# The down projection of an attention and feed-forward kernel: Strassen's seven products on 16 of its 22 inner tiles, instead of eight plain ones

## The chip, the core and the metric

One core of one Trainium2 chip. The metric is the device time of one execution in microseconds. Below, PE is TensorE, DVE is VectorE, ACT is ScalarE, POOL is GpSimd and SP is SyncE, which here only issues DMAs.

## The reference

```
xn = layernorm(x)                                    # x: 2 x 1024 tokens, width 1024, f32
s  = attention(xn, wq, wk, wv, wo)                   # 32 heads, 8 kv heads; s = (attended values) @ wo
w_gu, w_d = dequant(4-bit words, zeros, scales)      # 1024 x 5504 and 2752 x 1024
gate, up = split(xn @ w_gu)
h  = silu(gate) * up                                 # 2048 tokens x 2752
out = x + s * silu(h @ w_d)                          # h @ w_d is the down projection
```

## The kernel before, in words

Every f32 matrix product is done in f16 with each operand split into a high part and a low remainder: high x high, high x low and low x high, three matmuls of 128 x 128 by 128 x 512 where one would stand. All matmuls accumulate in PSUM in f32.

There are three stages. The first (`project_qkv`) normalises and projects; the second (`attend_and_expand`) does attention, dequantises, computes h and stores to scratch memory the transposed h (`ht_d`, f16 high and low), the dequantised w_d (`wd_d`, f16 high and low, 22 inner tiles of 128 rows, the last of 64) and the attention sums (`o_d`). The third is `finish`, the subject here. It loops over TT = 16 token tiles of 128 rows, the result of one being 128 x 1024 in two halves of BANK = 512 columns.

Each engine has its own program, executed in the order in which it is written out; semaphores are waited for with `wait_ge`. For token tile n (in the code m = n // 2, u = n % 2), `finish` does:

- DVE `dve_normalise` (L1820 to L1832): reciprocal of the row sums, an addition of the two parts of the attention sums, a multiplication, and a 32 x 32 block transposition. Then ACT `act_high` (L1770) makes the f16 high part of it, and DVE `dve_low` (L1841) the remainder.
- PE `project` (L1717): 8 inner tiles x 3 x 2 halves = 48 matmuls with wo. ACT `take` (L1786) brings the result from PSUM to SBUF, where it stays.
- PE `down` (L1731, L1726): for each half, 21 x 3 + 2 = 65 matmuls of h with w_d, which lies in SBUF as a whole (`wd_a` to `wd_e`).
- ACT `gate` (L1793): silu from PSUM. DVE `weigh` (L1859): times s. POOL `total` (L1899; for the last tile DVE, L1866): plus x. SP stores the half or the tile.

The order on PE: project 0, 1, 2; then the down products of tiles 0 and 1 inner tile by inner tile, while the weights arrive; project 3; and then in turn tile n (130 matmuls) and project n + 2 (48). So ACT and DVE prepare one projection in the time of 178 matmuls. `tail` puts the preparation of the first projections into the end of the second stage. All DMAs of the stage are issued by SP, in program order, each behind the waits ahead of it.

The buffers of `finish` lie in memory that the earlier stages used (`xT`, `stock`, `room`, `arena`), and two semaphore groups tell it when these are free: `units_done` and `units_stored`.

## Time and profile before

| | us |
|---|---|
| median of 3 runs | 2242.79 (2242.72 to 2243.02) |
| the profiled execution, own time | 2242.64 |
| its span | 2240.9 |
| TensorE busy | 2220.2 |
| VectorE busy | 1221.9 |
| GpSimd busy | 1200.0 |
| ScalarE busy | 930.6 |

The profile is one execution. Matmuls are pipelined, so that the duration of a single one (379 ns) is longer than the distance to the next; distances are read from blocks of them, count and time. A group's mean is over its instructions, and contains what they waited for while running. The chain of waits starts at the last instruction and goes back to what released each one.

### The profile page before, as it was taken

What the parts mean: (1) busy time and instruction counts of PE and PEld (TensorE: products, weight loads), DVE (VectorE), ACT (ScalarE), POOL (GpSimd) and SP (SyncE); (2) the same over time, 40 slices, a digit from 0 to 9 for tenths busy, and PEclk for the clock granted to TensorE, in tenths of its full rate; (3) what the DMA queues carried; (4) which work ended last, traced back from release to release, by engine and by line L of the source; (5) the groups of instructions that cost most, each with busy time, mean ns of one, the idle gap of its engine ahead of it and who ended that gap; (6) DMA issues with size and microseconds to landing.
All of it is one profiled execution on the core that took longest, in us unless ns stands there. A gap on an engine that the chain in (4) does not pass through costs nothing.

```text
span 2240.9 us, 38593 instructions
## 1 busy us (share of the span) xinstructions
PE 2220.2 (99%) x15048; PEld 1125.2 (50%) x15048; DVE 1221.9 (55%) x1951; ACT 930.6 (42%) x1806; POOL 1200.0 (54%) x1318
## 2 busy tenths in 40 slices
PE   7999999999999999999999999999999999999999
PEld 4555545555555555555555555444444444444444
DVE  5677677777777777777777763345312211112100
ACT  4333156666666666666666665332201000000000
POOL 4855588887887888788888876333301101001000
PEclk9999999999999999999999999999999999999999
DMA  7344212443424433334443233533273222313120
GB/s 208 97 105 100 50 33 57 72 76 55 67 59 81 72 67 59 67 62 72 76 61 61 66 53 61 94 103 92 81 295 127 100 91 77 113 64 127 45 89 19
DMA packets 266666, 188.03 MB, mean 84 GB/s; under 512 B 189728, under 2 KB 236318, under 8 KB 264052
## 3 DMA queue, kind: packets, MB, share of 16 engines
q1 hardware_dynamic: 266484, 185.56, 34.8%
q8 instruction: 119, 1.95, 0.4%
q14 instruction: 63, 0.52, 0.1%
HBM read 113.47 MB, written 71.90 MB: 83 GB/s over the span
## 4 chain that ended last, share of the span: by engine, by line
PE 98%; ACT 1%; DVE 0%; issue 0%; POOL 0%; DMA 0%; DVEq 0%; ACTq 0%; POOLq 0%
PE gu_ps L1174 39%; PE dn_ps L1731 19%; PE qk_ps L722 9%; PE out_ps L1717 7%; PE mx_ps L1071 6%; PE sc_ps L1115 6%; PE o_ps L1137 4%; PE v_ps L705 2%; PE o_ps L1141 2%; PE sz_ps L1084 2%; PE sz_ps L1089 1%; PE dn_ps L1726 1%; PE tr_ps L691 1%; ACT L1223 0%; POOL xl L412 0%
## 5 line engine op out<-in xcount | busy, mean ns | idle before, releaser
L1174 PE MATMUL gu_ps<-xT,wg 128*128 128x512 f16 x4128 | 983.6, 378 | 0.0
L1505 POOL TENSOR_TENSOR room<-room 128x1152 f16<-128x1152 f32 x256 | 539.5, 2107 | 40.3 <-ACT room L1223 26.4
L1174 PEld LDWEIGHTS gu_ps<-xT,wg 128*128 128x128 f16 x4128 | 367.8, 97 | 377.2 <-issue 0.7
L1223 ACT ACTIVATE room<-sc_ps 128x512 f32<-128x512 f32 (+3 forms) x768 | 349.3, 489 | 368.7 <-PE sc_ps L1115 365.0
L1731 PE MATMUL dn_ps<-xT,hT_in 128*128 128x512 f16 x1536 | 336.2, 379 | 0.0
L1899 POOL TENSOR_TENSOR room<-room 128x512 f32<-128x512 f32 x30 | 51.2, 1710 | 530.0 <-DVE room L1859 530.0
L1859 DVE TENSOR_TENSOR room<-room 128x512 f32<-128x512 f32 x32 | 23.9, 752 | 415.6 <-ACT room L1793 415.5
L1731 PEld LDWEIGHTS dn_ps<-xT,hT_in 128*128 128x128 f16 x1536 | 150.3, 98 | 181.2
L1500 POOL TENSOR_SCALAR_AFFINE_SELECT room<-room 128x128 f32<-128x128 f32 x512 | 144.8, 299 | 140.4 <-ACT room L1223 140.4
L1350 DVE TENSOR_REDUCE shift<-mx_ps 128x2 f16<-128x1024 f32 (+3 forms) x256 | 212.8, 831 | 8.8
L722 PE MATMUL qk_ps<-xT,w 128*128 128x512 f16 x960 | 212.8, 379 | 0.0
L1115 PE MATMUL sc_ps<-arena 97*128 97x512 f16 (+3 forms) x768 | 209.7, 327 | 2.3 <-ACT room L1223 2.1
L1350 DVE TENSOR_REDUCE part<-mx_ps 128x2 f16<-128x1024 f32 x128 | 157.1, 1227 | 100.3 <-PE mx_ps L1071 100.3
L1793 ACT ACTIVATE room<-dn_ps 128x512 f32<-128x512 f32 x32 | 19.0, 597 | 415.5 <-PE dn_ps L1726 415.2
L1137 PE MATMUL o_ps<-arena,room 128*128 128x65 f16 x2240 | 191.1, 191 | 0.0
L1071 PE MATMUL mx_ps<-arena 96*128 96x512 f16 (+3 forms) x768 | 188.0, 325 | 0.6 <-DVE shift L1350 0.6
L1141 PE MATMUL o_ps<-arena,room 128*128 128x33 f16 x2304 | 184.1, 178 | 0.0
L1137 PEld LDWEIGHTS o_ps<-arena,room 128*128 128x128 bf16 x2240 | 160.7, 97 | 32.4
L1717 PE MATMUL out_ps<-room,arena 128*128 128x512 f16 x768 | 168.1, 379 | 0.0
L1141 PEld LDWEIGHTS o_ps<-arena,room 128*128 128x128 f16 x2304 | 148.6, 96 | 37.5
L1345 DVE TENSOR_TENSOR mx_ps<-mx_ps,maskb 128x256 f32<-128x256 f32 x256 | 109.8, 429 | 79.5 <-PE mx_ps L1071 75.0
L1479 POOL TENSOR_TENSOR wg<-wf,wg 128x256 f16<-128x256 f32 (+1 forms) x176 | 120.6, 685 | 52.3 <-ACT wg L1199 52.3
(124 smaller groups left out, 2551.6 us busy)
## 6 DMA issues: line engine op xcount, KB each, us to landing
hidden_scratch<-hT SPq DMA_DIRECT2D x84, 256.0 KB, 3.0
hT_in<-hidden_scratch SPq DMA_DIRECT2D x16, 1344.0 KB, 6.0
o_scratch<-room SPq DMA_DIRECT2D x64, 260.0 KB, 10.4
room<-o_scratch SPq DMA_DIRECT2D x16, 1040.0 KB, 8.1
arena<-q_scratch SPq DMA_DIRECT2D x48, 256.0 KB, 3.8
stock<-in_qw_d SPq DMA_DIRECT2D x42, 256.0 KB
down_scratch<-wd SPq DMA_DIRECT2D x84, 128.0 KB, 2.8
xin<-in_x SPq DMA_DIRECT2D x16, 512.0 KB, 4.6
```

Source lines behind the costliest of these rows:

```text
L722: last = pe.matmul(qk_ps[bank_of(e)][:, :], w[:, wp, s, j * P:(j + 1) * P], xT[:, xp, s, tc * BANK:(tc + 1) * BANK], start=(s == 0 and k = ...
L1071: last = pe.matmul(mx_ps[:, e, 0:end - first], qT[0:STACK, u, q + e, t * P:(t + 1) * P], kT[0:STACK, u, first:end], start=True, stop=True)
L1115: last = pe.matmul(bank[:, 0:e - c], kT[0:STACK + 1, u, t * P:(t + 1) * P], qT[0:STACK + 1, u, q, c:e], start=True, stop=True)
L1137: pe.matmul(o_ps[:, c:c + VW], hi, vn[:, u, k, :], start=first, stop=False)
L1141: last = pe.matmul(o_ps[:, c:c + VH], lo, vn[:, u, k, 0:VH], start=False, stop=final)
L1174: last = pe.matmul(to[:, :], wg[:, u, wp, s, cols], xT[:, xp, s, tokens], start=(s == 0 and k == 0), stop=(s == KT - 1 and k == 2))
L1223: act.activation(probs[:, r % 2, START[t] + c:START[t] + e], sc_ps[n % SC_BANKS][:, 0:e - c], ACT.Exp, scale=float(1.0 / np.sqrt(HD))).the ...
L1350: dve.tensor_reduce(to, banks[:, :, 0:width], AX_X, ALU.max, negate=True).then_inc(mx_taken, 1)
L1500: pool.affine_select(out=block, in_=block, pattern=[[1, P]], compare_op=ALU.is_ge, fill=0.0, base=0, channel_multiplier=-1).then_inc(causa ...
L1505: pool.tensor_tensor(p_lo[:, r % 2, c], probs[:, r % 2, c], p_hi[:, r % 2, c], ALU.subtract).then_inc(lo_done, 1)
L1717: last = pe.matmul(out_ps[u][:, cols], aT[:, u, xp, s, :], w[:, wp, s, cols], start=(s == 0 and k == 0), stop=(s == KT - 1 and k == 2))
L1731: pe.matmul(dn_ps[u][:, half, :], hT[:, u, hp, j, :], src[:, wp, cols], start=(j == 0 and k == 0), stop=False)
```

## The change

Two token tiles, n1 = 2p and n2 = 2p + 1, now make a pair. The first 16 inner tiles of w_d are seen as 8 pairs of an even and an odd one. With h of the pair as A11 (n1, even), A12 (n1, odd), A21 and A22 (n2), and w_d as B11, B12 (even tiles, left and right columns), B21, B22 (odd), the four quarters of the result are formed from seven products of 8 inner tiles x 3 matmuls, each 128 x 512 (M1 to M7), in place of eight. The other six inner tiles are multiplied as before (`rest`), 17 matmuls for each quarter, and stand first in a pair, ahead of the products M3, M1, M5, M7, M6, M4, M2.

- Five of the seven weight operands are sums or differences of blocks of w_d: 40 items (8 inner pairs x 5 kinds) of 128 x 512. Each is made on chip from four f16 parts: DVE adds the high parts, POOL the low parts (`item_rest`), DVE (even items) or POOL (odd items) adds the two, ACT takes the f16 high part, POOL the remainder (`item_low`), and SP stores it to the new scratch `ws_d`. The sources come from `wd_d` as 8 loads of 1 MB into the one buffer `src`. The seven operands are then loaded as whole blocks of 2 MB.
- Five of the seven h operands are sums too, made for each pair: `sum_tiles`, three DVE operations of 128 x 1024 into the one buffer `t`, an ACT copy (high part) and a POOL subtraction (remainder) into a ring of three.
- The results of the products are brought together by ACT copies and ten DVE additions from PSUM per pair.
- All 16 projections come first, with the items between them (`items(n)`: 2, 3, 3 in turn). Their results go to the new scratch `s_d` and are loaded again for `weigh` tile by tile (`load_last`), with x, into single buffers. PE begins pair 0 when `last_zeroed` is 2, which DVE sets after all 40 items are stored.
- h now has three buffers, and `total` for a pair is interleaved with the remainders on POOL.

The core of the diff; between the lines shown are removed lines, helpers for addresses, `free` (a wait until the PSUM bank is read), and the memory plan:

```diff
+        def items(n):
+            return range(min(ITEMS, 8 * n // 3), min(ITEMS, 8 * (n + 1) // 3))
...
+            def load_source(i):
+                if i >= PAIRS:
+                    return
+                if i >= 1:
+                    g = SUMS * i - 1
+                    sp.wait_ge(bsum_done[g % 2], g // 2 + 1)
+                    sp.wait_ge(bsum_done[1 - g % 2], (g - 1) // 2 + 1)
+                sp.dma_start(src[:, :, :, :].rearrange("p h e c -> p h (e c)"),
+                             wd_d[:, :, 2 * i * D:2 * (i + 1) * D]).then_inc(b_loaded, 16)
+            def store_item(g):
+                sp.wait_ge(bl_done, g + 1)
+                sp.dma_start(ws_d[g % SUMS, :, :, g // SUMS, :], ob[:, g % 2, :, :]).then_inc(b_stored[g % 2], 16)
...
+            def load_last(n):
+                if n >= TT:
+                    return
+                if n >= 1:
+                    sp.wait_ge(sum_done, 2 * n)
+                    sp.wait_ge(prod_done, 2 * n)
+                sp.dma_start(xs[:, :], x_v[n]).then_inc(x_loaded, 16)
+                for half in range(2):
+                    sp.dma_start(s_in[half], s_d[n, :, half * BANK:(half + 1) * BANK]).then_inc(s_loaded, 16)
...
             for n in range(TT):
+                load_sums(sp, n + 4)
+                if n >= 1:
+                    store_sums(n - 1)
+                for g in items(n):
+                    if g % SUMS == SUMS - 1:
+                        load_source(g // SUMS + 1)
+                    store_item(g)
+            for q in range(2):
+                sp.wait_ge(b_stored[q], 16 * ITEMS // 2)
+            load_block(B_M3)
+            load_block(B_M1)
+            sp.wait_ge(a_turned, TT)
+            load_block(B_M4)
+            store_sums(TT - 1)
+            sp.wait_ge(out_ready, TT)
+            load_block(B_M7)
+            load_block(B_M6)
+            load_whole(B_M2, 0, 0)
+            for q in range(2):
+                sp.wait_ge(so_stored[q], 16 * TT // 2)
...
+            def rest(n, half, to, first, final):
+                cols, h = slice(half * BANK, (half + 1) * BANK), hT[n % 3]
+                for j in range(FTILES - 1 - PLAIN):
+                    for k, (hp, wp) in enumerate([(0, 0), (0, 1), (1, 0)]):
...
+            def product(to, stationary, kind, first=True, final=True):
+                for i in range(PAIRS):
+                    for k, (hp, wp) in enumerate([(0, 0), (0, 1), (1, 0)]):
+                        last = pe.matmul(to, stationary(hp, i), blocks[kind][:, wp, i, :],
+                                         start=(first and i == 0 and k == 0),
...
+            def pair(p):
+                n1, n2, e, q = 2 * p, 2 * p + 1, 5 * p, SUMS * p
...
+                    pe.wait_ge(added, 10 * (p - 1) + 5)
+                rest(n1, 0, c_ps[C11], True, False)
+                rest(n1, 1, c_ps[C12], True, True).then_inc(k_done, 1)
...
+                    pe.wait_ge(added, 10 * (p - 1) + 8)
+                rest(n2, 0, c_ps[C21], True, True).then_inc(k_done, 1)
+                rest(n2, 1, c_ps[C22], True, False)
...
+                free(e)
+                product(m_bank(e), lambda hp, i: hT[n1 % 3][:, hp, 2 * i, :], B_M3)
...
+                free(e + 1)
+                product(m_bank(e + 1), summed(q), B_M1)
...
+                free(e + 2)
+                product(m_bank(e + 2), summed(q + 1), B_M5)
...
+                product(c_ps[C11], summed(q + 2), B_M7, first=False)
...
+                product(c_ps[C22], summed(q + 3), B_M6, first=False)
...
+                free(e + 3)
+                product(m_bank(e + 3), lambda hp, i: hT[n2 % 3][:, hp, 2 * i + 1, :], B_M4)
...
+                free(e + 4)
+                product(m_bank(e + 4), summed(q + 4), B_M2)
...
+            for n in range(3):
+                project(n)
             units_done(pe)
+            for n in range(3, TT):
+                project(n)
             pe.wait_ge(last_zeroed, 1)
...
+            pe.wait_ge(wk_loaded, 16)
+            pe.wait_ge(tail_loaded, 32)
+            pe.wait_ge(last_zeroed, 2)
+            for p in range(DP):
+                pair(p)
...
+            def item_high(g):
+                act.wait_ge(bsum_done[g % 2], g // 2 + 1)
+                if g >= 2:
+                    act.wait_ge(b_stored[g % 2], 16 * (g // 2))
+                act.activation(ob[:, g % 2, 0, :], bt[:, g % 2, :], ACT.Copy).then_inc(bh_done, 1)
...
+            def pair(p):
+                q = SUMS * p
+                copy(p, 0, C12)
+                copy(p, 0, C22)
+                copy(p, 1, C11)
+                sum_high(q + 3)
+                gate(p, C12, 4)
+                sum_high(q + 4)
+                sum_high(q + 5)
+                sum_high(q + 6)
+                copy(p, 3, C21)
+                gate(p, C11, 7)
+                gate(p, C21, 9)
+                gate(p, C22, 10)
+                sum_high(q + 7)
...
+                if n >= 1:
+                    act_high(act, n + 1)
+                    take(n - 1)
+                for g in items(n):
+                    item_high(g)
...
+            def item(g):
+                first, second, op = of_item(g)
+                dve.wait_ge(b_loaded, 16 * (g // SUMS + 1))
+                if g >= 2:
+                    dve.wait_ge(bl_done, g - 1)
+                dve.tensor_tensor(bt[:, g % 2, :], quarter(0, first), quarter(0, second), op).then_inc(bt_done, 1)
+                if g % 2 == 0:
+                    dve.wait_ge(bu_done, g + 1)
+                    dve.wait_ge(bt_done, g + 1)
+                    dve.tensor_tensor(bt[:, g % 2, :], bt[:, g % 2, :], bu[g % 2], ALU.add
+                                      ).then_inc(bsum_done[0], 1)
+            def sum_tiles(q):
+                if q >= SUMS * DP:
+                    return
+                first, second, op = of_sum(q)
+                for n in (first[0], second[0]):
+                    dve.wait_ge(ht_loaded[n % 3], 48 * (n // 3 + 1))
+                if q >= 1:
+                    dve.wait_ge(comb_lo, q)
+                dve.tensor_tensor(t[:, :, :], tiles(0, first), tiles(0, second), op).then_inc(comb_step, 1)
+                dve.wait_ge(comb_step, 3 * q + 1)
+                dve.tensor_tensor(t[:, :, :], t[:, :, :], tiles(1, first), ALU.add).then_inc(comb_step, 1)
+                dve.wait_ge(comb_step, 3 * q + 2)
...
+            def pair(p):
+                q, n1, n2 = SUMS * p, 2 * p, 2 * p + 1
+                dve.wait_ge(m_done, 7 * p + 2)
+                dve.wait_ge(copied, 4 * p + 3)
+                add(p, 1, C22, of_m(p, 1), ALU.add)
+                sum_tiles(q + 3)
+                dve.wait_ge(m_done, 7 * p + 3)
+                add(p, 2, C11, of_m(p, 2), ALU.subtract)
+                add(p, 3, C12, of_m(p, 2), ALU.add)
+                dve.wait_ge(k_done, 2 * p + 1)
+                add(p, 4, C12, c_ps[C12], ALU.add)
+                sum_tiles(q + 4)
+                dve.wait_ge(m_done, 7 * p + 4)
+                add(p, 5, C11, c_ps[C11], ALU.add)
+                sum_tiles(q + 5)
+                sum_tiles(q + 6)
+                dve.wait_ge(m_done, 7 * p + 5)
+                add(p, 6, C22, c_ps[C22], ALU.add)
+                dve.wait_ge(m_done, 7 * p + 6)
+                dve.wait_ge(copied, 4 * p + 4)
+                add(p, 7, C11, of_m(p, 3), ALU.add)
+                dve.wait_ge(k_done, 2 * p + 2)
+                add(p, 8, C21, c_ps[C21], ALU.add)
+                weigh(n1, 1)
+                weigh(n1, 0)
+                dve.wait_ge(m_done, 7 * p + 7)
+                add(p, 9, C21, of_m(p, 4), ALU.add)
+                add(p, 10, C22, of_m(p, 4), ALU.subtract)
+                for half in range(2):
+                    weigh(n2, half)
+                    if n2 == TT - 1:
+                        total(n2, half)
+                sum_tiles(q + 7)
...
+            for n in range(TT):
+                if n >= 1:
+                    dve_low(dve, n + 1)
+                if n >= 2:
+                    dve_normalise(dve, n + 2)
+                for g in items(n):
+                    item(g)
+            dve.wait_ge(bl_done, ITEMS)
+            for q in range(2):
+                dve.wait_ge(b_stored[q], 16 * ITEMS // 2)
+            dve.memset(h_third[FLAST:P, 1, FTILES - 1, :], 0.0).then_inc(last_zeroed, 1)
...
+            def item_rest(g):
+                first, second, op = of_item(g)
+                pool.wait_ge(b_loaded, 16 * (g // SUMS + 1))
+                if g >= 2:
+                    pool.wait_ge(bsum_done[g % 2], g // 2)
+                pool.tensor_tensor(bu[g % 2], quarter(1, first), quarter(1, second), op).then_inc(bu_done, 1)
+            def item_low(g):
+                if g % 2:
+                    pool.wait_ge(bt_done, g + 1)
+                    pool.wait_ge(bu_done, g + 1)
+                    pool.tensor_tensor(bt[:, g % 2, :], bt[:, g % 2, :], bu[g % 2], ALU.add
+                                       ).then_inc(bsum_done[1], 1)
+                pool.wait_ge(bh_done, g + 1)
+                pool.tensor_tensor(ob[:, g % 2, 1, :], bt[:, g % 2, :], ob[:, g % 2, 0, :], ALU.subtract
+                                   ).then_inc(bl_done, 1)
...
+            def pair(p):
+                q, n1, n2 = SUMS * p, 2 * p, 2 * p + 1
+                for k in range(3, 7):
+                    sum_low(q + k)
+                total(n1, 1, 1)
+                total(n1, 0, 2)
+                if n2 < TT - 1:
+                    total(n2, 0, 1)
+                    total(n2, 1, 2)
+                sum_low(q + 7)
+            for g in range(ITEMS):
+                if g % SUMS == 0 and g:
+                    item_low(g - 1)
+                item_rest(g)
+                if g % SUMS and g:
+                    item_low(g - 1)
```

## Rows read from the trace of the kernel before

**Rows 1.** The page's busy line and GpSimd's 40 slices.

```profile
PE 2220.2 (99%) x15048; PEld 1125.2 (50%) x15048; DVE 1221.9 (55%) x1951; ACT 930.6 (42%) x1806; POOL 1200.0 (54%) x1318
...
POOL 4855588887887888788888876333301101001000
```

**Rows 2.** The chain that ended last, in order: start, us, engine and line.

```profile
1621.44 31.19 PE out_ps L1717 x144
...
1747.16 10.36 PE out_ps L1717 x48
...
2235.80 0.45 PE dn_ps L1726 x2
...
2237.73 0.69 DVE room L1866
```

**Rows 3.** Groups by line and form, whole span: busy us, mean ns, idle before.

```profile
L1443 DVE SCALAR_TENSOR_TENSOR h<-gu_ps,h 128x512 f32<-128x512 f32 x84 | 57.9, 690 | 73.7 <-PE gu_ps L1174 73.7
...
L1859 DVE TENSOR_TENSOR room<-room 128x512 f32<-128x512 f32 x32 | 23.9, 752 | 415.6 <-ACT room L1793 415.5
...
L1832 DVE STREAM_TRANSPOSE arena<-room 128x1024 f32<-128x1024 f32 x16 | 19.9, 1245 | 0.5
L1841 DVE TENSOR_TENSOR arena<-arena 128x1024 f16<-128x1024 f32 x16 | 19.6, 1224 | 85.8 <-ACT arena L1770 85.8
...
L1519 POOL TENSOR_TENSOR hT<-h,hT 128x512 f16<-128x512 f32 x84 | 97.6, 1162 | 55.7 <-ACT hT L1264 55.7
...
L412 POOL TENSOR_TENSOR xl<-xn,xh 128x1024 f16<-128x1024 f32 x16 | 38.1, 2383 | 43.0 <-ACT xh L477 42.9
...
L1264 ACT ACTIVATE hT<-h 128x512 f16<-128x512 f32 x84 | 52.7, 627 | 32.9 <-DVE h L1443 32.1
...
L1770 ACT ACTIVATE arena<-arena 128x1024 f16<-128x1024 f32 x16 | 16.8, 1047 | 0.0
```

**Rows 4.** Timeline of VectorE at 1633 and 2094: start, us, operation.

```profile
1633.39 0.17 DVE L1871 MEMSET hT_in<- 64x128 uint32 x1 [1.32 <-DMA down_scratch<-wd]
...
2094.20 0.35 DVE L1820 RECIPROCAL rsum<-room 128x32 f32<-128x32 f32 x1
2094.46 1.16 DVE L1821 TENSOR_TENSOR room<-room 128x1024 f32<-128x1024 f32 x1
2095.73 2.10 DVE L1825 TENSOR_TENSOR room<-room,rsum 128x1024 f32<-128x1024 f32 x1
```

**Rows 5.** Timeline of GpSimd there and at 2132.

```profile
2094.36 2.38 POOL L1899 TENSOR_TENSOR room<-room 128x512 f32<-128x512 f32 x1 [12.69 <-DVE room L1859]
...
2132.78 1.26 POOL L1899 TENSOR_TENSOR room<-room 128x512 f32<-128x512 f32 x1 [12.70 <-DVE room L1859]
```

**Rows 6.** Timeline of VectorE from 700 to 716.

```profile
702.06 1.54 DVE L1369 TENSOR_SCALAR stock<-stock 128x256 uint32<-128x256 uint32 x1
...
710.62 0.28 DVE L1369 TENSOR_SCALAR stock<-stock 128x256 uint32<-128x256 uint32 x1
```

**Rows 7.** Timeline of GpSimd there.

```profile
701.35 2.11 POOL L1505 TENSOR_TENSOR room<-room 128x1152 f16<-128x1152 f32 x1 [0.24 <-ACT room L1223]
```

**Rows 8.** VectorE's group of line 1353.

```profile
L1353 DVE TENSOR_TENSOR shift<-shift,part 128x8 f16<-128x8 f16 x32 | 25.3, 792 | 1.1
```

**Rows 9.** DMA issues from 1600 on: count, KB, median us to landing.

```profile
hT_in<-hidden_scratch SPq DMA_DIRECT2D x16, 1344.0 KB, 6.0
...
hidden_scratch<-hT SPq DMA_DIRECT2D x1, 256.0 KB, 3.0
```

**Rows 10.** Total of the DMA packets from 1640 to 1662.

```profile
DMA packets 2469, 8.95 MB, mean 407 GB/s; under 512 B 351, under 2 KB 351, under 8 KB 2468
```

**Rows 11.** Timeline of TensorE at the start.

```profile
16.23 7.27 PE L705 MATMUL v_ps<-w,xT 128*128 128x256 f16 x48
...
26.69 5.40 PE L705 MATMUL v_ps<-w,xT 128*128 128x256 f16 x48
```

**Rows 12.** Stretch of the last 5 us: busy of five engines, clock, DMA.

```profile
2236.00:2241.00 5.00, 0.24 (x2) 0.00 (x0) 1.39 (x2) 0.60 (x1) 0.00 (x0) 0.77 0.14 52
```

More of the change, by code:

```diff
@@ new lines, in quarter, with of_sum, tiles @@
+        def quarter(h, at_block):
+            e, half = at_block
+            return src[:, h, e, half * BANK:(half + 1) * BANK]
+        def of_sum(q):
+            p, kind = q // SUMS, q % SUMS
+            n1, n2 = 2 * p, 2 * p + 1
+            first = [(n1, 0), (n1, 0), (n1, 1), (n2, 0), (n2, 0)][kind]
+            second = [(n2, 1), (n1, 1), (n2, 1), (n1, 0), (n2, 1)][kind]
+            return first, second, ALU.subtract if kind in (2, 3) else ALU.add
+        def tiles(h, at_block):
+            n, e = at_block
+            return hT[n % 3][:, h, 0:PLAIN, :].rearrange("p (i e) k -> p i e k", e=2)[:, :, e, :]
@@ L1890, in vector @@
[L1890 to L1909 removed]
+            dve.memset(h_two[FLAST:P, :, 1, FTILES - 1, :], 0.0).then_inc(last_zeroed, 1)
```

460 lines of the change are left out of this document (252 added, 208 removed).

## The prediction

> **What bounds the kernel now.** I read the page's busy line and slices first: TensorE is busy 99% of the span, the other engines about half, and in the last quarter the digits of GpSimd sink to 1 and 0 [rows 1]. Then the chain that ended last, from the first projection (1621.44) on: whole blocks of 48 projection and 65 down matmuls, each starting where the one before ends, up to 2236.25; behind the last come a gate, a product and a sum, some 2.2 us, and the store [rows 2]. So the stretch is a count of matmuls: 48 in 10.36 us are 0.2159 us each, and 768 + 2080 of them make 614.8 us, the distance from 1621.44 to 2236.25. A matmul taken out there is worth its 0.2159 us as long as TensorE never waits. Third, the durations and interference on the engines that get new work [rows 3 to 9]. My sum is made on the profiled execution, 2242.6 us (span 2240.9, 1.7 around it), 0.2 below the median.
>
> **TensorE's part.** A pair of token tiles took 4 x 65 = 260 matmuls. Now the six rest tiles take 4 x 17 = 68 and seven products of 8 x 3 take 168: 236, or 50.9 us. Eight pairs save 192 matmuls, **-41.4 us**.
>
> **What must be done before the first pair.** Projection no longer alternates with the down products: all 16 projections come first, and pair 0 waits (last_zeroed) until all 40 sums of weight blocks are built and stored. With nothing late the projections would end at 1621.4 + 16 x 10.36 = 1787.2. The question is whether VectorE, ScalarE and GpSimd build 40 sums, 2.67 per projection, in that time, with the normalising of the attention sums (which they did before too, but at one tile in 38.4 us).
>
> Prices. GpSimd, 128x512: 1.15 us to f16, 1.27 to f32; a sum has one f32 rest, every second one an f32 addition, all one f16 remainder: 1.27 + 0.63 + 1.15 = 3.05. VectorE, 128x512 from SBUF: 0.69, starting 0.61 to 0.65 apart in a row; 1.5 of them, 0.98. ScalarE 0.63. A projected tile needs on VectorE 0.35 + 1.16 + 1.2 (undisturbed) + 1.25 to normalise and transpose, 1.23 for the low part, on ScalarE 1.05 and about as much for the result [rows 3 to 5]. Without a row are only sources that are both f16; I price them like f32, since with one f16 source or output 128x512 and 128x1024 keep near 2.3 ns an element on GpSimd, as with f32 alone. Below, they could cost half, above a quarter more.
>
> Interference decides. The sum L1899 on GpSimd takes 1.26 us alone, but 2.38 when L1821 on VectorE (1.16) starts beside it; the next VectorE operation then takes 2.09 instead of about 1.2, its excess being what was left of the GpSimd one [rows 4, 5]. Elsewhere L1369 takes 0.28 alone and 1.54 beside a GpSimd operation that ends just before it does [rows 6, 7]; VectorE operations that read PSUM keep their time: L1443 takes 0.69 in the mean of 84, spread over the stretch in which GpSimd is busy eight tenths [rows 1, 3]. So the two engines take turns when both read only SBUF. All of the new preparation reads only SBUF.
>
> The Trainium skill (SBUF — State Buffer, section "SBUF: two separate sides") says that VectorE with two SBUF inputs and GpSimd hold a shared port pair for a whole instruction each, and names no type. The rows agree for f32 (1.26 and 2.38 us); by the rule the f16 sources are no exception and the sum below stands; without it for them, it would be that of the first rival.
>
> The walk. Each engine works in program order: VectorE's iteration is low part (behind ScalarE's copy, which is behind the last item's copy), normalise, then items; there are two buffers, so GpSimd can run only two rests and one remainder ahead. Per eight items (three iterations) the turns are, on GpSimd, 8 x (1.27 + 1.15) + 4 x 1.27 = 24.4; on VectorE 12 x 0.65 = 7.8 and 3 x (1.23 + 1.16 + 1.2) = 10.8: 43.0 us. To these come times in which neither can use its turn: the transposition (1.25) when GpSimd has run out of allowed work, and ScalarE's copy with its hand-overs (0.8) ahead of the remainder, about 1.9 per iteration, 5.7. So 48.7 per three, **16.2 us an iteration** against 10.36 of projection. From there:
> - VectorE enters at 1633.4 (its memset [rows 4]); the first 1 MB source lands 5.2 later (between 256 KB in 3.0 and 1344 KB in 6.0, nearer the larger [rows 9]): 1638.6.
> - Iterations 0 and 1 (five items, one low part): 20 us, 1659. Projection 2 already starts late.
> - Iterations 2 to 13: 12 x 16.2 = 195, 1854.
> - The source has one buffer. Its load is issued after the last reader (and on SP behind the store of the item before), 5.2 us plus issue; seven reloads, two at an iteration's beginning, where the normalising hides all but 1.5, two that cost 4.5 and three (even items) some 6: 28 taken (10 to 35), 1882.
> - Iteration 14 has no normalising: 11.5. Last remainder 2, last store 3 (a 256 KB store took 3.0 [rows 9]): **T0 = 1898**.
> Projection k is released by iteration k-1, so projections stretch along and the last ends about 1850 to 1890, before T0. T0 - 1787 = **+111 us** in which TensorE idles, in pieces of some 6 us and one longer.
>
> **From T0 on.** TensorE begins with 14.7 us of rest products, whose weights are in. Meanwhile 12 MB of blocks must come: the tall window moves 407 GB/s [rows 10], 2.1 MB in 5.2 us, so products needed at T0 + 14.7, 20, 25, 30, 36, 41, 46 find them; bounds 0 and +10 us, I take 0. Sums of h: three VectorE operations of 1.16 to 1.23, a copy of 1.05, a remainder of 2.2 (2.38 the nearest, a 128x1024 [rows 3], shortened for disturbance), 7.1 us with hand-overs, one at a time. With T the end of M1: sum 3 is there at T + 8.5 (needed T + 10.4), sum 4 at 15.6 (20.7), sum 5 at 22.7, sum 6 at 29.8, addition 8, for which the next pair's third rest product waits, at 29.5 (33.2), sum 7 about 46 (56). Additions from PSUM cost 0.69 (L1443 [rows 3]) and take no turns. All fit, narrowest by 2 us; a pair stays 50.9 us, eight 407.4.
> **Clock**: granted 1.00 throughout, but 0.77 in the last 5 us, after TensorE stopped; at the start, after a wait, 48 products take 7.27 and the next 48 of the kind 5.40 [rows 11, 12]. Coming back from the lower level (1.2 GHz) costs about 1.9 us by that row; I add **+2** at T0, and nothing in the projections, which aren't last there.
> **The end**: behind the last matmul 4.65 us today. Now M2 feeds two additions (1.3) and two gates (0.6 each, in row), while x and the stored projection of the last tile are loaded only after the sums of the tile before (GpSimd, T + 26.2), landing some 5 us later (T + 31.5, matmuls end T + 25.9); then two products, two sums, a store: about 11. **+6**. Bounds +3 and +9.
>
> Sum: 2242.6 - 41.4 + 111 + 2 + 6 = **2320 us**, which is T0 + 422.1.
>
> **Rivals.**
> 1. The turns don't bind the f16 operations. An iteration is then VectorE's own order: 7.1 for copy, copy, low part and normalising, plus 5.7 for the items: 12.8. 12 x 3.4 less: **2279**. For it: no row with two f16 sources in large. Against: eight columns of f16 (L1353, both SBUF) take 0.79 us in the mean, which only waiting explains [rows 8].
> 2. The other side: preparation keeps pace. GpSimd's own work is 40 x 3.05 = 122 us, less than 1787 - 1639 = 148; if VectorE's share slips between and reloads hide, T0 = 1793 and the time is **2215**. It decides at T0 = 1820.5, where T0 + 422.1 is today's time, that is 12.1 us an iteration with no reload showing. Against: even VectorE's order without turns gives 12.8, and reloads are waited for.
> 3. The clock stays at the lower level through the broken-up projections. 48 x 0.43 = 20.7 is more than an iteration's 16.2: 13 of them from 1652 set T0 at about 1928: **2350**. By the Trainium skill (TensorE: Matmul & The Clock Gate, section "Part 1: The HAM clock gate") idle time gives the lower level and sustained work returns the full one; [rows 11] agree with the return, which makes this unlikely.
> 4. The pairs aren't bound by TensorE: sums of h late, 60 us a pair, +72: **2390**. For it: two margins of 2 to 4 us. Against: the walk above.
>
> **Numbers.** Forecast 0.60 (its own range 2295 to 2345), rival 1 0.17, rival 2 0.12, rival 3 0.05, rival 4 0.04, no change 0.02. The range 2262 to 2350 holds the forecast's case, rival 3 and most of rival 1, about 8 in 10. 0.2% of the time, 4.5 us, is about what a measurement can tell. Only rival 2 is faster, with the low edge of rival 1: faster 0.13, same 0.03, slower 0.84.
>
> **What would show it.** TensorE idle before the projections, 6 us each, from projection 2 on; a wait for last_zeroed ending near 1898; GpSimd's 128x512 operations near 1.9 us in the mean in that stretch, not 1.2; then products without a gap, 51 us a pair, and 11 us behind them. Wrong would be shown by projections on a 10.4 us beat, by 12.8 us iterations, by the clock below 1.00 throughout a projection, or by gaps inside pairs.

## The result and the profile after

| | before | after |
|---|---|---|
| median (lowest to highest), us | 2242.90 (2242.72 to 2243.02) | 2332.53 (2331.45 to 2333.41) |
| ratio, 95% interval | | 1.0399 (1.0381 to 1.0417) |
| profiled execution, own time; span, us | 2242.6; 2240.9 | 2332.88; 2331.1 |
| TensorE matmuls, mean granted clock | 15048, 1.00 | 14856, 0.979 |

The change costs 89.6 us. The forecast was 2320 with a range of 2262 to 2350. The page of the kernel after; its busy line and GpSimd's slices answer to [rows 1]:

```profile
PE 2200.6 (94%) x14856; PEld 1110.0 (48%) x14856; DVE 1489.4 (64%) x2212; ACT 1012.5 (43%) x1918; POOL 1415.4 (61%) x1458
...
PE   7999999999999999999999999999666579999997
...
POOL 4755687878878787887878863333454442333332
...
PEclk9999999999999999999999999999878899999999
```

TensorE falls to between 5 and 7 tenths in five slices, where before it was full (9) in all of them; the 192 matmuls are gone. TensorE's waits from 1600 on (waiting for: total, times, longest):

```profile
PE out_ps L1810 <- DVE arena L2010: 95.9, 13, 13.7
PE dn_ps L1819 <- DVE room L2117: 2.8, 1, 2.8
PE dn_ps L1819 <- DVE room L2053: 2.2, 1, 2.2
PE dn_ps L1830 <- POOL xT L2145: 0.4, 1, 0.4
```

The projections (L1810) wait 13 times for the low part of their operand (L2010) on VectorE, the first rest product (L1819) 2.8 us for the gate behind the last stored sum (L2117), and the pairs 2.6 us in all. TensorE's timeline, which answers to the chain of [rows 2]:

```profile
1649.48 12.80 PE L1810 MATMUL out_ps<-room,arena 128*128 128x512 f16 x48 [7.07 <-DVE arena L2010]
1671.96 11.82 PE L1810 MATMUL out_ps<-room,arena 128*128 128x512 f16 x48 [9.67 <-DVE arena L2010]
...
1720.28 13.24 PE L1810 MATMUL out_ps<-room,arena 128*128 128x512 f16 x48 [6.35 <-DVE arena L2010]
1746.58 12.05 PE L1810 MATMUL out_ps<-room,arena 128*128 128x512 f16 x48 [13.06 <-DVE arena L2010]
...
1893.16 12.15 PE L1810 MATMUL out_ps<-room,arena 128*128 128x512 f16 x48 [8.68 <-DVE arena L2010]
1908.09 3.40 PE L1819 MATMUL dn_ps<-xT,hT_in 128*128 128x512 f16 x15 [2.79 <-DVE room L2117]
...
2315.70 2.97 PE L1830 MATMUL out_ps<-arena,xT 128*128 128x512 f16 x13
```

So T0, the start of pair 0, is 1908.1 (forecast 1898), the matmuls end 2318.7, and 12.4 us of tail follow. T0 and the low parts of VectorE give the rate. Its timeline (the low parts are L2010; between the one at 1669.78, where iteration 2 begins, and the one at 1891.16 lie twelve iterations):

```profile
1638.83 0.69 DVE L2028 TENSOR_TENSOR room<-room 128x512 f32<-128x512 f16 x1 [5.14 <-DMA room<-down_scratch]
...
1648.05 1.33 DVE L2010 TENSOR_TENSOR arena<-arena 128x1024 f16<-128x1024 f32 x1 [5.25 <-ACT arena L1912]
1649.31 1.63 DVE L2028 TENSOR_TENSOR room<-room 128x512 f32<-128x512 f16 x1
...
1651.65 0.68 DVE L2028 TENSOR_TENSOR room<-room 128x512 f32<-128x512 f16 x1
...
1669.78 1.89 DVE L2010 TENSOR_TENSOR arena<-arena 128x1024 f16<-128x1024 f32 x1 [1.64 <-ACT arena L1912]
...
1739.48 0.69 DVE L2028 TENSOR_TENSOR room<-room 128x512 f32<-128x512 f16 x1 [10.99 <-DMA room<-down_scratch]
...
1891.16 1.89 DVE L2010 TENSOR_TENSOR arena<-arena 128x1024 f16<-128x1024 f32 x1 [1.64 <-ACT arena L1912]
...
1907.72 0.11 DVE L2117 MEMSET room<- 64x64 uint32 x1 [6.87 <-DMA down_sum_scratch<-arena]
```

(1891.16 - 1669.78) / 12 = 18.45 us an iteration, reload waits included, such as the 10.99 us at 1739. The forecast had 16.2 plus 28/12, 18.5. GpSimd's timeline at the same place answers to [rows 5]:

```profile
1638.88 1.66 POOL L2129 TENSOR_TENSOR room<-room 128x512 f32<-128x512 f16 x1 [9.03 <-DMA room<-down_scratch]
1640.50 1.15 POOL L2129 TENSOR_TENSOR arena<-room 128x512 f32<-128x512 f16 x1
...
1648.26 2.13 POOL L2129 TENSOR_TENSOR arena<-room 128x512 f32<-128x512 f16 x1
```

These are the rows that the kernel before lacked. With two f16 sources a 128x512 takes GpSimd 1.15 us alone. At 1648.26 it starts while VectorE's L2010 (f32 sources) still runs, and takes 2.13; VectorE's L2028 (f16 sources) starts beside it at 1649.31 and takes 1.63 instead of 0.68. At 1638.8 both are of the kind with two f16 sources: VectorE, 0.05 us ahead, takes its 0.69, and GpSimd 1.66. Whichever starts second is longer by about what was left of the other. The groups from 1634 on answer to [rows 3] (busy, mean ns; idle before):

```profile
L2138 POOL TENSOR_TENSOR arena<-room,arena 128x512 f16<-128x512 f32 x40 | 49.4, 1237 | 76.5 <-ACT arena L1932 76.5
...
L2028 DVE TENSOR_TENSOR room<-room 128x512 f32<-128x512 f16 x40 | 36.6, 926 | 70.8 <-DMA room<-down_scratch 51.0 <-POOL arena L2138 19.7
...
L2129 POOL TENSOR_TENSOR arena<-room 128x512 f32<-128x512 f16 x20 | 30.9, 1544 | 24.8 <-DMA room<-down_scratch 24.8
...
L1932 ACT ACTIVATE arena<-room 128x512 f16<-128x512 f32 x40 | 24.6, 630 | 225.0 <-POOL room L2135 121.4 <-DVE room L2032 88.0 <-DMA down_sum_scratch<-arena 15.6
...
L1925 ACT ACTIVATE room<-out_ps 128x1024 f32<-128x1024 f32 x16 | 16.1, 1003 | 0.0
```

Turns are there, but the means are 1.2 to 1.5 us, not 1.9; VectorE waits 51.0 us for the source (room<-down_scratch), and ScalarE's copy waits mostly for the sums. ScalarE's copy of a projection's result (L1925) never waited for TensorE. Of the 51.0 us, 5.1 are the first load; the seven reloads are the rest, by VectorE's waits from 1640 to 1908:

```profile
DVE room L2028 <- DMA room<-down_scratch: 45.9, 7, 11.0
```

Windows over this stretch and behind it (us, busy of PE, PEld, DVE, ACT and POOL, granted clock, DMA share, GB/s); the last answers to [rows 12]:

```profile
1720.00:1760.00 40.00, 25.43 (x97) 10.34 (x98) 18.28 (x20) 6.78 (x9) 20.39 (x15) 0.76 0.46 140
...
1908.00:1960.00 52.00, 51.91 (x241) 23.60 (x242) 25.17 (x23) 9.56 (x11) 11.21 (x6) 1.00 0.85 329
2319.00:2331.00 12.00, 0.00 (x0) 0.00 (x0) 3.76 (x6) 1.26 (x2) 0.24 (x1) 0.67 0.51 175
```

### The profile page after: what moved, and what is told of

Its sections match the earlier page's. It is cut to its first block, busy times and chain, and to the rows that moved or that the text cites. A ratio compares the mean times of both kernels' runs of the same rounds, so it can differ in the third digit from the quotient of the medians.

```text
span 2331.1 us, 39206 instructions
## 1 busy us (share of the span) xinstructions
PE 2200.6 (94%) x14856; PEld 1110.0 (48%) x14856; DVE 1489.4 (64%) x2212; ACT 1012.5 (43%) x1918; POOL 1415.4 (61%) x1458
## 4 chain that ended last, share of the span: by engine, by line
PE 82%; issue 7%; POOL 5%; DVE 3%; DMA 2%; ACT 2%; SPq 0%; POOLq 0%; DVEq 0%; ACTq 0%
PE gu_ps L1178 38%; PE qk_ps L726 9%; PE out_ps L1830 7%; PE mx_ps L1075 6%; PE sc_ps L1119 5%; PE dn_ps L1819 4%; PE o_ps L1141 4%; PE dn_ps L1830 3%; PE o_ps L1145 2%; PE v_ps L709 2%; PE sz_ps L1088 2%; POOL arena L2138 1%; POOL arena L2129 1%; POOL room L2135 1%; PE sz_ps L1093 1%
## 5 line engine op out<-in xcount | busy, mean ns | idle before, releaser
L1810 PE MATMUL out_ps<-room,arena 128*128 128x512 f16 x768 | 187.8, 410 | 95.9 <-DVE arena L2010 95.9
L2145 POOL TENSOR_TENSOR xT<-arena,xT 128x1024 f16<-128x1024 f32 x40 | 85.1, 2128 | 210.7 <-ACT xT L1940 210.7
L1810 PEld LDWEIGHTS out_ps<-room,arena 128*128 128x128 f16 x768 | 78.7, 104 | 204.8 <-issue 129.0
L1940 ACT ACTIVATE xT<-arena 128x1024 f16<-128x1024 f32 x40 | 42.3, 1057 | 283.4 <-DVE arena L2047 277.3
L726 PEld LDWEIGHTS qk_ps<-xT,w 128*128 128x128 f16 x960 | 93.5, 98 | 107.8 <-issue 0.3
L1523 POOL TENSOR_TENSOR hT<-h,hT 128x512 f16<-128x512 f32 (+1 forms) x88 | 102.6, 1165 | 67.0 <-ACT hT L1268 67.0
```

The lines of the kernel that those rows point to most:

```text
L726: last = pe.matmul(qk_ps[bank_of(e)][:, :], w[:, wp, s, j * P:(j + 1) * P], xT[:, xp, s, tc * BANK:(tc + 1) * BANK], start=(s == 0 and k = ...
L1810: last = pe.matmul(out_ps[u][:, cols], aT[:, u, xp, s, :], w[:, wp, s, cols], start=(s == 0 and k == 0), stop=(s == KT - 1 and k == 2))
```

## The experiments

Twelve kernels, each beside the kernel before on the same chip. "T0" is the start of the first rest product; "an iteration" is the mean of the twelve between the same two low parts as above.

**e1_no_items: is it the sums at all?** The 40 sums, their stores and the loads of their sources are left out; the blocks are loaded from the plain weights.

```diff
 def load_source(i):
+    return
 def store_item(g):
+    return
-sp.dma_start(blocks[kind][:, :, :, :], ws_d[kind])
+sp.dma_start(blocks[kind][:, :, :, :], wd_d[:, :, 0:PAIRS * BANK] ...)
```

> The changed kernel without the making of the 40 weight sums: their additions, copies, remainders, stores and the eight source loads are left out, and the five blocks are loaded from the dequantised weights in the same size. Theory (the preparation sets the start of pair 0, and all else is as it was): projections on a 10.4 us beat, the last ends near 1788, pair 0 begins there; 1788 + 424.8 (what the changed kernel needs from its pair 0, at 1908.1, to its time of 2332.9) = 2213 us. Rival (the projections are slowed by TensorE's own clock or by the loads, or the pairs carry the loss): over 2290.

Measured 2215.5 us (2215.1 to 2216.3), ratio 0.9878 (0.9863 to 0.9893). T0 is 1794.6, with one gap of 4.1 us in the projections and none in the pairs, and T0 to the end takes 421.0. So the whole loss is the preparation: of the 117.0 us between the two kernels 113.5 are T0. From T0 to the end of the last matmul it takes 407.7 us, so the count of matmuls is right.

**e2_psum_operand: what do the turns cost?** The second operand of VectorE's operations of the preparation comes from PSUM (a constant, so values aren't the reference's).

```diff
-dve.tensor_tensor(bt[:, g % 2, :], quarter(0, first), quarter(0, second), op)
+dve.tensor_tensor(bt[:, g % 2, :], quarter(0, first), c_ps[0], op)
...   (likewise the addition, the low part and both operations of the normalising)
```

> In the changed kernel, VectorE's two-input operations of the preparation (normalising, low part, items) take their second operand from PSUM instead of SBUF, at the same size and in the same order; the values are not the reference's. Theory (VectorE and GpSimd take turns at SBUF, f16 sources included): GpSimd's 128x512 operations fall from 1.4 to 1.5 us in the mean to 1.15 to 1.26, VectorE's from 0.93 and 1.25 to 0.69, the iteration by about 3.4 us, the time by 41 us to 2290 (2280 to 2305). Rival (program order and loads set the pace, the turns only fill idle time): 2325 to 2333.

Measured 2313.7 us (2311.7 to 2314.1), ratio 1.0316. Groups from 1634 on, which answer to L2129, L2028 and L2010 above:

```profile
L2034 DVE TENSOR_TENSOR room<-room,dn_ps 128x512 f32<-128x512 f16 x40 | 26.7, 674 | 73.6 <-DMA room<-down_scratch 48.6 <-POOL arena L2148 25.0
...
L2139 POOL TENSOR_TENSOR arena<-room 128x512 f32<-128x512 f16 x20 | 23.1, 1153 | 23.3 <-DMA room<-down_scratch 23.3
...
L2015 DVE TENSOR_TENSOR arena<-arena,dn_ps 128x1024 f16<-128x1024 f32 x14 | 17.1, 1221 | 60.2 <-ACT arena L1914 60.2
```

Every stretched duration fell to its undisturbed value (1544 to 1153, 926 to 674, 1453 to 1221 ns), so the mechanism is shown, for f16 too. But the kernel gained 19 us, half of what the forecast's walk asks and less than was expected: an iteration went from 18.45 to 16.93. Over both engines the operations of the preparation became 49 us shorter in total, and T0 fell by 20.6; the remainder had filled time in which the engine would have waited anyway.

**e3_two_sources: the reloads.** The source has two buffers (in the area where block M5 was loaded early; M5's load goes behind the others).

```diff
-src = shape(room[:, made[1]:made[2]], F16, "p (h e c) -> p h e c", h=2, e=2)
+src = shape(stock[:, :], F16, "p (u h e c) -> p u h e c", u=2, h=2, e=2)
-load_source(g // SUMS + 1)
+load_source(g // SUMS + 2)
```

> The changed kernel with two source buffers for the weight sums, in the memory of M5's block, which is now loaded with the other blocks behind pair 0's start. Theory (each reload of the single source is waited for): seven waits go, 28 us by my sum, and some 5 more of the crowd of loads at the beginning: 2300 us (2292 to 2312). Rival (the waits are time in which the engines catch up with work they owe anyway): 2320 or more.

Measured 2300.8 us (2300.4 to 2301.5), ratio 1.0258, as expected. T0 fell by 38.5 us to 1869.6, an iteration to 15.54, and the time by 31.7. Of the 38.5, 34.9 lie in the twelve iterations; iteration 2 began 3.6 us earlier, with M5's load out of the way. What T0 gained and the time didn't shows in TensorE's waits and its first rest products:

```profile
PE out_ps L1811 <- DVE arena L2011: 57.1, 13, 7.1
...
PE dn_ps L1820 <- DVE room L2054: 5.7, 1, 5.7
```

```profile
1869.60 5.08 PE L1820 MATMUL dn_ps<-xT,hT_in 128*128 128x512 f16 x15 [1.96 <-DVE room L2118]
```

With the load of M5 (2 MB) now behind T0, pair 1 waits 5.7 us instead of 2.2. And TensorE wasn't at its full clock at T0: 15 matmuls took 5.08 us where the kernel after had 3.40 (granted clock 0.84 in the first 10 us, 1.00 there), and 4.74 behind the wait in pair 1. T0 to the end takes 431 instead of 424.8: 3.5 us of the difference are the wait and 3.0 the clock.

**e4_rest_early: the gate.** Pair 0's rest products don't use the sums; they start ahead of the wait.

```diff
-pe.wait_ge(last_zeroed, 2)
+if p == 1:
+    pe.wait_ge(last_zeroed, 2)
```

> The changed kernel with TensorE's wait for the last stored item moved from ahead of pair 0 to ahead of pair 1, so that pair 0's 68 rest products (14.7 us) run before it. Theory (they need nothing of the items, and M3 can start when its block has been loaded, about 7.5 us after the last store): 7 us gained, 2326 us. Rival (the last projection is so late that nothing is left to gain, or the first sums of h come later than the blocks): 2331 to 2333.

Measured 2333.0 us (2331.9 to 2335.2), ratio 1.0402: nothing gained. TensorE and ScalarE at T0:

```profile
1904.52 3.40 PE L1819 MATMUL dn_ps<-xT,hT_in 128*128 128x512 f16 x15
...
1920.61 1.67 PE L1830 MATMUL out_ps<-xT,hT_in 128*128 128x512 f16 x7 [1.25 <-ACT room L1926]
...
1967.60 4.88 PE L1819 MATMUL dn_ps<-xT,hT_in 128*128 128x512 f16 x15 [3.24 <-DVE room L2054]
```

```profile
1911.33 1.06 ACT L1941 ACTIVATE xT<-arena 128x1024 f16<-128x1024 f32 x1 [6.99 <-DVE arena L2048]
1918.50 1.06 ACT L1941 ACTIVATE xT<-arena 128x1024 f16<-128x1024 f32 x1 [6.11 <-DVE arena L2048]
1919.46 1.00 ACT L1926 ACTIVATE room<-out_ps 128x1024 f32<-128x1024 f32 x1
```

The rest products began 3.6 us earlier, not more, since the last projection had ended only then; and M3, which reuses the banks of the last projection, waited for L1926, which frees them. ScalarE has that copy in its program behind two copies (L1941) of the sums of h, whose additions on VectorE stand behind the same gate. M3 still began 2.2 us earlier than in the kernel after. Pair 1 took that back: its wait was 3.2 us instead of 2.2, and the 15 matmuls behind it took 4.88 us instead of 3.40. The waits moved; my expectation overlooked the late projection and a third engine's order.

**e5_loads_later: the jam at the start.** e3, with the loads of the hidden tiles and of the kept blocks at iterations 4, 6 and 8 instead of at the beginning.

```diff
-load_hidden(0)
-load_hidden(1)
 for n in range(TT):
+    if n == 4:
+        load_hidden(0)
+    if n == 6:
+        load_hidden(1)
```

> The kernel with two source buffers (2300.8 us), and the loads of the first two tiles of h and of the kept weights moved behind iterations 4, 6 and 8 of the preparation. Theory (the first stores of items queued behind these loads, ScalarE waited 13 us for them, and so iteration 2 began 11 us later than in my walk): 2291 us (2288 to 2294). Rival (the jam is made up later, since the iterations after it have slack): 2298 or more.

Measured 2297.0 us (2295.7 to 2298.1), ratio 1.0241, short of what was expected. What e3 (L1716, the load of M5) and this one (L1756, the tail of the kept blocks) take off the queue, and ScalarE beside it, in the kernel after:

```profile
1639.34 8.62 SPq L1716 DMA_DIRECT2D stock<-down_scratch  x1
1648.00 4.91 SPq L1756 DMA_DIRECT2D wd_c<-down_scratch  x2
...
1653.59 1.24 SPq L1711 DMA_DIRECT2D down_sum_scratch<-arena  x2
```

```profile
1662.96 0.63 ACT L1932 ACTIVATE arena<-room 128x512 f16<-128x512 f32 x1 [14.03 <-DMA down_sum_scratch<-arena]
```

The issues of these early loads occupied the queue for 13.5 us, the first finished sum was stored only from 1653.6, and ScalarE waited 14 us for its buffer. Without them iteration 2 began at 1659.0 instead of 1666.2 (e3), 7.3 us earlier, but the twelve iterations took 15.80 instead of 15.54 each, 3.1 us back, so T0 gained 4.2 and the time 3.8 us. The 3.1 us are the moved loads themselves: iteration 4 took 17.5 us instead of 16.4 and iteration 8, with the kept blocks, 19.5 instead of 16.9. There ScalarE again waited for a store, in this kernel:

```profile
1771.27 0.63 ACT L1939 ACTIVATE arena<-room 128x512 f16<-128x512 f32 x1 [8.30 <-DMA down_sum_scratch<-arena]
```

**e6_both: do they add?** e3 and e2 together (e2's values).

```diff
-dve.tensor_tensor(bt[:, g % 2, :], quarter(g, 0, first), quarter(g, 0, second), op)
+dve.tensor_tensor(bt[:, g % 2, :], quarter(g, 0, first), c_ps[0], op)
```

> The kernel with two source buffers, and VectorE's second operands from PSUM as well (values are not the reference's). The two edits alone saved 31.7 and 18.9 us. Theory (turns and reloads are separate costs, and program order is the rest): 2282 us (2276 to 2288). Rival, my walk (12.8 us an iteration without turns, against 15.5 measured between the projections of the two-source kernel): 2268. Rival (without the waits for reloads there is no idle time left for the turns to hide in, so they cost more): 2265 or less.

Measured 2286.8 us (2286.1 to 2288.1), ratio 1.0196. The turns now cost 14.0 us (19 alone): nearly additive. ScalarE waited 37.8 us, 8 times, for stores, against 13.0 us, 3 times, in e3: the two buffers of finished parts hold it up more often now.

**e7_six_slots: the stores.** e6 with six buffers of finished parts instead of two.

```diff
-ob = shape(arena[:, spare + BANK:spare + 3 * BANK], F16, "p (u h c) -> p u h c", u=2, h=2)
+ob = [... for area, k in ((arena[:, spare + BANK:spare + 3 * BANK], 2), (room[:, made[1]:made[2]], 4)) for s in range(k)]
-act.wait_ge(b_stored[g % 2], 16 * (g // 2))
+act.wait_ge(b_stored[g % SLOTS], 16 * (g // SLOTS))
```

> The kernel with two source buffers and VectorE's second operands from PSUM (2286.8 us; values are not the reference's), with six buffers for the finished parts of a sum instead of two. In its trace ScalarE waited 37.8 us for stores of such parts to land. Theory (what was left above my walk of 12.8 us an iteration, 14.65 measured, is these stores): 12 x 1.85 = 22 us less, 2265 (2260 to 2272). Rival (program order and hand-overs, the store waits run beside them): 2280 or more.

Measured 2270.7 us (2269.9 to 2271.3), ratio 1.0123: 16 us less. T0 fell by 17.3 us, of which 10.6 lie ahead of iteration 2, where the early loads had held up the first stores (1655.9 instead of 1666.5), and only 6.9 in the twelve iterations, where I had expected all of it. With no turns, no reload wait and no store wait in its way an iteration still takes 14.08 us, against 10.36 of projection. I take that as the order of the engines' programs; the forecast had 12.8 for it.

**e8_six_slots_turns: the same with turns.** e5 with six buffers.

```diff
-act.wait_ge(b_stored[g % 2], 16 * (g // 2))
+act.wait_ge(b_stored[g % SLOTS], 16 * (g // SLOTS))
```

> The kernel with two source buffers and later loads (2297.0 us, all operands where the change has them), with the six buffers. Theory (with turns the iterations are slow enough that stores mostly land in time, ScalarE waits 12.5 us for them): 5 to 12 us less, 2288. If the turns are a cost of their own, it stays some 20 us above the kernel with operands from PSUM and six buffers: 20 is the measured price of the turns then.

Measured 2292.9 us (2292.6 to 2293.1), ratio 1.0222. The buffers give only 4.2 us here, 3.8 of it in the iterations (15.48 instead of 15.80): the jam at the start, the larger part of what they gave in e7, e5 had already taken away. e8 less e7, 22.2 us, prices the turns once more, with a reserve: e7 has the early loads and e8 the later ones, and what these are worth beside six buffers no run shows. In the twelve iterations the two differ by 16.8 us, ahead of them by 2.9, behind them by 2.3.

**w1_tensor_sums: give half of the sums to TensorE.** e5 and e4, with every even item summed in PSUM by four products with the identity or its negative; ScalarE and VectorE split it from there. On VectorE the odd items go ahead of the normalising, and ScalarE frees the banks of the last projection first.

```diff
+for i, (by, h, of) in enumerate([(ident[:, :], 0, first), (ident[:, :], 1, first),
+                                 (sign, 0, second), (sign, 1, second)]):
+    last = pe.matmul(c_ps[g // 2 % 4], by, quarter(g, h, of), start=(i == 0), stop=(i == 3))
...
+take(TT - 1)
 for q in range(2):
     sum_high(q)
-take(TT - 1)
```

> A kernel with all of this taken up: two source buffers; loads later; TensorE makes every second weight sum by four products with the identity (or its negative) into the PSUM banks that pair 0 does not need yet, ScalarE and VectorE take its parts from PSUM, so 20 sums ask no turns; VectorE issues the other items ahead of the normalising; TensorE starts pair 0's rest products before the last item, and ScalarE takes the last projection before it copies sums of h. TensorE pays 80 x 0.216 = 17.3 us. Theory (the preparation, not TensorE, set pair 0's start): projections and sums on a beat of 11.5 us, pair 0 begins near 1807, and 1807 + 424.8 = 2232 us, faster than before by 0.5%. Rival (program order between ScalarE and VectorE still takes 13 us an iteration): 2250. Rival (the early rest products only move the wait to product M3): up to 8 us more, 2240.

Measured 2283.3 us (2282.7 to 2285.2), ratio 1.0181, 51 us from what I expected. Its waits from 1600 on:

```profile
ACT arena L1961 <- DMA down_sum_scratch<-arena: 119.8, 18, 14.2
PE out_ps L1819 <- DVE arena L2043: 24.6, 6, 6.5
...
PE dn_ps L1915 <- DMA stock<-down_scratch: 10.5, 3, 3.9
```

The sums were no longer what was waited for: ScalarE stood before its two output buffers for 120 us. I had looked at the adding engines alone.

**w2_last_ahead: the tail.** w1, with x and the stored projection of the last tile loaded at the start of the last pair into a spare area.

```diff
+if p == DP - 1:
+    load_xs(TT - 1)
```

> The same, and x and the stored projection of the last token tile are loaded at the beginning of the last pair into the buffer of h that is free by then. Theory (the last tile's loads were issued only after the sums of the tile before and ended 5 us after its gates): 5 us less than the kernel without it, about 2227 us. Rival (the gates and additions behind the last matmul are the chain anyway): no difference.

Measured 2276.6 us (2276.1 to 2277.6), ratio 1.0151: 6.8 us less. In the traces the time behind the last matmul fell from 12.7 to 6.9 us, so 5.8 are the tail's wait for its loads; T0 was 2.6 us earlier in this execution, which the edit doesn't explain.

**w3_six_slots: all together.** w2 with the six buffers, TensorE's sums behind the projection of their iteration.

```diff
-    items_summed(n)
     project(n)
+    items_summed(n)
```

> The kernel in which TensorE makes every second sum and the last tile's loads go ahead (2276.6 us), with six buffers for the finished parts, and TensorE's sums of an iteration behind its projection instead of ahead of it. In its trace ScalarE waited for the stores, TensorE 24.6 us for VectorE's low parts and 10.5 us for sources. Theory (both waits go back to stores behind SP's other loads): TensorE's beat is 11.5 us, pair 0 begins near 1810, 2230 us, faster than before by 0.5%. Rival (VectorE's own order, 6.2 us of preparation with turns and the sums, is over 12 us an iteration): 2245 to 2260, no gain over before.

Measured **2225.3 us** (2224.4 to 2225.3), ratio **0.992** (0.9905 to 0.9935): below the kernel before. A window, and TensorE's timeline:

```profile
1660.00:1740.00 80.00, 80.00 (x372) 36.26 (x371) 61.91 (x54) 25.61 (x35) 45.62 (x29) 1.00 0.93 323
```

```profile
1656.16 10.52 PE L1839 MATMUL out_ps<-room,arena 128*128 128x512 f16 x48
1666.52 1.03 PE L1935 MATMUL dn_ps<-stock,ident 128*128 128x512 f16 x4
1667.38 10.52 PE L1839 MATMUL out_ps<-room,arena 128*128 128x512 f16 x48
```

TensorE is busy for all 80 us at full clock, a sum (L1935) in 0.86 us between projections. T0 is 1804.65; full projections plus 80 sum matmuls of 0.2159 give 1787.2 + 17.3 = 1804.5. GpSimd's rests and additions, 128x512, still take 1.5 to 1.8 us in the mean: the turns are there, and up to T0 TensorE doesn't wait for them.

**e9_all_but_tensor_sums: which part does it?** e8 with e4's gate, ScalarE's order of w1 and w2's tail, that is w3 without the sums on TensorE (and without the order on VectorE that goes with them).

The cut is from the difference to w3:

```diff
-project(0)
-project(1)
+for n in range(3):
+    project(n)
...
-items_summed(0)
-items_summed(1)
-for n in range(2, TT):
+for n in range(3, TT):
     project(n)
-    items_summed(n)
```

> The fast kernel (2225.3 us) without its main part: TensorE makes no weight sums, VectorE and GpSimd make all 40 as in the change, with the reordering that goes with it left out; kept are two source buffers, six slots, later loads, the early rest products, the last projection taken first and the last tile's loads ahead. Theory (the shared turns and VectorE's order bind, 15 us an iteration in the kernel with six slots and turns): 2292.9 less 5 for the rest products and 6 for the tail, 2281 (2276 to 2286), so that TensorE's 17 us of sums buy 55. Rival (the small edits did most of it): 2250 or less.

Measured 2284.6 us (2284.3 to 2285.2), ratio 1.0186. So TensorE's 17.3 us of sums, together with the order on VectorE that goes with them, buy 59 us, and without both the rest is worth 8.2 us over e8.

## Why the prediction was right

The direction, the cause and the size of 2320 held (89.6 us slower, 77 forecast). The size owes something to luck: several terms missed and offset one another. The first column is the step's.

| step | forecast | measured |
|---|---|---|
| matmuls removed | 192 | 192 |
| iteration 2 begins | 1659 | 1669.8 |
| twelve iterations, reloads included | 223 | 221.4 |
| from there to T0 | 16.5 | 16.9 |
| T0 | 1898 | 1908.1 |
| pairs | 407.4 | 410.6 |
| clock coming back at T0 | 2 | 0 |
| behind the last matmul | 10.7 | 12.4 |

- **TensorE's part**: right. In e1, where nothing waits in the pairs, they take 407.7 us; forecast 407.4.
- **The twelve iterations**: 223 forecast, 221.4 measured, but by parts that missed both ways. The forecast was 154 of program order, 41 of turns and 28 of reloads. Along the kernels that were run it is 169.0 of program order (e7), 16.8 of turns (e8 less e7, with the loads moved), 3.8 of stores (e5 to e8), 3.1 less for the moved loads (e3 to e5) and 34.9 of reloads (to e3). That the sum agrees within 2 us is luck.
- **Price of the turns**: over-sized. 3.4 us an iteration, 41 us, were taken; measured 19 (e2), 14 (e6) and about 22 (e8 less e7, which has the moved loads in it too). Turns exist as walked (2.13 us where 1.15 is the undisturbed time), but the walk made both engines' turns one sum, as if neither had slack; they had, since ScalarE and the source were waited for too. Means of 1.9 on GpSimd were my sign for it, and 1.2 to 1.5 stood there.
- **Program order**: under-sized. 12.8 us an iteration without turns in the walk, 14.08 in e7.
- **Reloads**: 28 taken from 10 to 35 (the parts that I listed add to 30); e3 gives 34.9 us in the iterations, 38.5 of T0 and 31.7 of time. Both the sum of their waits in the kernel after (45.9 us on VectorE) and this say that I should have gone to the upper end.
- **Stores**: missed. I counted only the last one (3 us). Two buffers with a 2.6 us landing look ample, but a store stands behind 1 and 2 MB loads in one queue: 14 us of ScalarE's time at the start, where iteration 2 began 11 us late. Six buffers took 10.6 us off the start and 6.9 off the iterations without turns (e6 to e7), and 3.8 off the iterations with turns (e5 to e8), the start having been cleared before.
- **Sum of the parts**: from after to e1 T0 falls by 113.5 us: 38.5 reloads (e3), 4.2 early loads (e5), 3.7 stores (e8), 22.0 turns (e7), 45.1 left for the program order. The step to e7 also puts the loads back to the start. The forecast's split of its 111 was 28, 0, 0, 41 and the rest. The steps overlap, so another sequence would share them out otherwise; this one is the one that was run.
- **Clock**: to add nothing in the projections was right in effect, but incomplete. The granted clock was 0.76 to 0.90 in the windows from 1640 to 1908, a mean of the two levels, 1.2 and 2.4 GHz, and 48 matmuls took up to 13.2 us instead of 10.5; but ScalarE's copies of the results never waited (L1925, 0.0), and the last projection ended 2.8 us before T0, so T0 didn't move. That margin was small: I had the last projection end at 1850 to 1890, and it ended at 1905. The Trainium skill (TensorE: Matmul & The Clock Gate, section "Part 1: The HAM clock gate") lets idle time lower the clock and sustained work restore it; the windows agree, 0.76 with gaps of 6 to 13 us and 1.00 behind T0. My +2 at T0 measured 0 in this kernel, where the rest products ran at once in 3.40 us for 15 behind a gap of 2.8 us. It isn't wrong as a price: in e3, behind a gap of 2.0 us, the same 15 took 5.08, and behind the gaps in pair 1 they took 4.74 (e3) and 4.88 (e4) us. When it must be paid these runs don't settle.
- **Pairs**: one wait of 2.2 us in pair 1 and one of 0.4. The first is the third rest product waiting for addition 8 of pair 0, to which I had given a margin of 3.7 us, not for the sum with the narrowest, 2. VectorE was late for it because a tile of h was:

```profile
1954.53 1.23 DVE L2043 TENSOR_TENSOR arena<-room,hT_in 128x1024 f32<-128x1024 f16 x1 [8.38 <-DMA hT_in<-hidden_scratch]
```

Loads in the crowd behind T0 took up to 17.1 us (2 MB) and 20.6 (1 MB) in the median of their group to land; my walk had priced the blocks of weights and not the tiles of h behind them. Zero from bounds of 0 and 10 was nearly right here, and wrong in e3 (5.7).
- **Tail**: its mechanism is shown by w2, 5.8 us behind the last matmul.
- **Rival 1** (turns don't bind f16) fell by the rows at 1638.8 and 1648.3; and with no turns at all e2 takes 2314, not 2279. **Rival 2** (preparation keeps pace) needed 12.1 an iteration; even e7 misses that. **Rival 3** (clock) would have needed projections longer than an iteration, and they took 13.2 of 18.45; its own sum, 13 times 20.7 from 1652, gives 1921 and not 1928. **Rival 4** (60 us a pair) fell by 410.6 / 8 = 51.3.

Not settled: which hand-over makes program order 14.08 rather than 12.8, since no kernel changed VectorE's order alone. The trace of e7 names the chain: VectorE's low parts wait 60.1 us for ScalarE's copy ahead of them, and ScalarE's copies of the sums wait 90.0 us for GpSimd's additions and 66.6 for VectorE's. A split of TensorE's sums from that reordering in w3 wasn't tried either.

## What to carry to other kernels

Work taken from the binding engine pays only if what prepares it keeps its beat: 192 matmuls are worth 41 us, and their preparation, on engines that the page showed half idle, put off the start of the pairs by 113. Divide the busy time that a change adds to each engine by the stretch in which it must be done, then walk the chain through every engine's program order with its buffers, the output buffers of stores too; a limit taken away uncovers the next (w2 with two output buffers 1.015, w3 with six, and TensorE's sums behind the projection, 0.992). Where the preparing engines are late by more than the binding one would need to do part of the work itself, let it: 17 us of identity products, with the reordering on VectorE, bought 59.

## What the hardware did that was not expected

- GpSimd and VectorE take turns with f16 sources as with f32: 1.15 alone, 1.66 behind an f16 operation of VectorE and 2.13 behind an f32 one; VectorE 0.68 and 1.63. The Trainium skill (SBUF — State Buffer, section "SBUF: two separate sides") gives the lock without a type, and these rows agree. One PSUM operand on VectorE's side took all of it away here (e2: 1153 and 674 ns in the mean).
- Stretched operations need not stretch the kernel: in w3 they did on GpSimd (1.5 to 1.8 us in the mean), and TensorE was busy throughout from 1660 to 1740.
- Issuing loads took SP's own time: 8.62 and 4.91 us for three loads at 1639, behind 7 MB of loads issued since 1633, where single issues just before and behind them take 0.3 to 0.7.
